# Three 256-column matmuls into one set of columns in the second layer of a two-layer block with experts

## The reference, cut to what matters

```python
h = gelu(einsum('bnd,hd->bnh', x, fc1_w) + fc1_b)
shared = einsum('bnh,sh->bns', h, fc2_w) + fc2_b
We = experts_w[indices]                      # one of 16 experts for each row
be = experts_b[indices]
expert_x = einsum('bnh,bph->bnp', h, We) + be[:, None, :]
out = x + concatenate([shared, expert_x], axis=-1)
```

## Time and profile before

| | |
|---|---|
| Three executions | 381.62, 382.38, 383.69 us |
| Span of the profiled execution (first to last instruction) | 380.7 us |
| TensorE (PE) matmuls busy | 368.8 us, 97% of the span, 1841 matmuls |
| TensorE weight loads (PEld) | 309.5 us, 1841 loads |
| VectorE (DVE) | 217.0 us, 57% |
| ScalarE (ACT) | 196.5 us, 52% |
| GpSimd (POOL) | 57.1 us, 15% |
| Mean granted TensorE clock | 0.985 |

### The profile page before, as it was taken

How to read it: one execution, slowest core, us unless ns; L and a number is a source line. 1 busy time by engine, 2 the same in 40 slices (tenths; PEclk the granted TensorE clock), 3 DMA queues, 4 the chain that set the end, 5 groups by cost and what they waited for, 6 DMA issues and landing times.

```text
span 380.7 us, 5936 instructions
## 1 busy us (share of the span) xinstructions
PE 368.8 (97%) x1841; PEld 309.5 (81%) x1841; DVE 217.0 (57%) x331; ACT 196.5 (52%) x266; POOL 57.1 (15%) x27
## 2 busy tenths in 40 slices
PE   4799999999999999999999999999999999999996
PEld 4587877888888888888888888888888888888885
DVE  1289477656556556655655665565565566556442
ACT  2297356555554655555455454546546554653520
POOL 1023121230120303012030300203030030302000
PEclk9599999999999999999999999999999999999999
DMA  6932987444240523324052441415234151300011
GB/s 137 250 77 85 305 149 196 144 104 126 60 141 26 140 88 96 131 58 143 27 133 94 96 131 46 127 54 134 94 89 138 43 130 55 89 28 29 28 37 47
DMA packets 64516, 39.08 MB, mean 103 GB/s; under 512 B 37338, under 2 KB 63722, under 8 KB 64506
## 3 DMA queue, kind: packets, MB, share of 16 engines
q1 hardware_dynamic: 63584, 35.41, 34.1%
q0 software_dynamic: 880, 3.54, 3.6%
q10 hardware_dynamic: 42, 0.00, 0.0%
HBM read 27.40 MB, written 8.39 MB: 94 GB/s over the span
## 4 chain that ended last, share of the span: by engine, by line
PE 86%; DVE 5%; DMA 5%; ACT 2%; SPq 2%; issue 1%
PE fc_ps L593 40%; PE acc_ps L629 29%; PE acc_ps L631 15%; DMA resid<-in_L_cond_fc_w 2%; DVE ht L466 2%; DMA pieces<-in_L_cond_experts_w 2%; SPq L174 1%; ACT ht L343 1%; PE fc_ps L601 1%; DVE tr_ps L411 1%; PE fc_ps L565 1%; ACT gelu L338 0%; SPq L218 0%; DVE xt L404 0%; ACT w2t L305 0%
## 5 line engine op out<-in xcount | busy, mean ns | idle before, releaser
L593 PE MATMUL fc_ps<-xt,w1t 128*128 128x512 f32 x762 | 194.2, 394 | 0.0
L629 PE MATMUL acc_ps<-w2t,ht 128*128 128x512 f32 x512 | 185.1, 398 | 1.3 <-DVE resid L485 0.8
L593 PEld LDWEIGHTS fc_ps<-xt,w1t 128*128 128x128 f32 x762 | 135.6, 188 | 28.8
L466 DVE TENSOR_TENSOR ht<-gelu,ht 128x1024 fp32r<-128x1024 f32 x64 | 83.2, 1301 | 130.2 <-ACT ht L343 130.2
L338 ACT ACTIVATE gelu<-fc_ps,b 128x512 f32<-128x512 f32 x128 | 88.2, 690 | 131.5 <-PE fc_ps L593 127.8
L631 PE MATMUL acc_ps<-w2t,ht 128*128 128x256 f32 x512 | 143.5, 280 | 0.0
L629 PEld LDWEIGHTS acc_ps<-w2t,ht 128*128 128x128 f32 x512 | 96.2, 188 | 26.0 <-DVE w2t L404 1.8
L631 PEld LDWEIGHTS acc_ps<-w2t,ht 128*128 128x128 f32 x512 | 96.6, 189 | 3.9
L260 POOL TENSOR_TENSOR resid<-x_in,bias 128x1024 f32<-128x1024 f32 x16 | 51.0, 3190 | 282.0 <-DMA out<-resid 251.5
L343 ACT ACTIVATE ht<-gelu 128x1024 fp32r<-128x1024 f32 x64 | 67.9, 1062 | 2.0
L481 DVE TENSOR_TENSOR resid<-acc_ps,resid 128x256 f32<-128x256 f32 x64 | 26.8, 419 | 7.5 <-PE acc_ps L631 7.5
(11 more groups left out here) (27 smaller groups left out, 35.3 us busy)
## 6 DMA issues: line engine op xcount, KB each, us to landing
x_in<-in_x SPq DMA_DIRECT2D x16, 512.0 KB, 4.6
pieces<-in_L_cond_experts_w SPq DMA_DIRECT2D x128, 64.0 KB, 2.0
out<-resid SPq DMA_DIRECT2D x30, 256.0 KB, 2.2
pieces<-in_x SPq DMA_DIRECT2D x56, 128.0 KB, 2.8
w2t<-w2t POOLq DMA_DIRECT2D x4, 768.0 KB, 8.6
resid<-in_L_cond_fc_w SPq DMA_DIRECT2D x8, 128.0 KB, 7.0
bias<-in_L_cond_experts_b SPq DMA_DIRECT2D x32, 32.0 KB, 3.5
pieces<-in_L_cond_fc_w SPq DMA_DIRECT2D x4, 192.0 KB, 4.9
```

The lines of the kernel that those rows point to most:

```text
L466: nc.vector.tensor_tensor(ht[:, par, LO, 2 * r:2 * r + 2, :].rearrange("p k t -> p (k t)"), gelu[:, r % 2, :], ht[:, par, HI, 2 * r:2 * r ...
L593: last = nc.tensor.matmul(fc1_ps[:, j % FC1_BANKS, :], w1t[:, d, w, js], xt[:, par, d, v, :], start=(at == 0), stop=(at == len(terms) - 1))
L629: nc.tensor.matmul(acc_ps[:, bank, :], ht[:, par, HI, k, ts], w2t[:, par, t // T, k, :], start=(k == 0), stop=False)
```

## The change

The second layer no longer uses two sets of columns. For each token tile and chunk three matmuls of 256 columns (HI by HI, HI by LO, LO by HI) add into columns 0 to 255 of the bank. The columns multiplied for a chunk stay 512 + 256 = 3 x 256. One addition instead of two drains a tile, and the semaphore between the two additions goes. VectorE gets waits on its own semaphore `tr_lo` ahead of the transposes into `tr_ps` in `step`; they ask for remainders computed earlier on the same engine.

```diff
@@ tile_out
                 dve.wait_ge(acc_filled, 1 + q + 1)
                 if t == 0:
                     dve.wait_ge(resid_ready, i + 1)
-                nc.vector.tensor_tensor(dst, acc_ps[:, bank, OUT:2 * OUT], dst, ALU.add)\
-                    .then_inc(cross_added, 1)
-
-                dve.wait_ge(cross_added, q + 1)
                 nc.vector.tensor_tensor(dst, acc_ps[:, bank, 0:OUT], dst, ALU.add)\
                     .then_inc(acc_drained, 1)
@@ step of VectorE
                     if r == 0 and x_ahead:
+                        dve.wait_ge(tr_lo, x_at(i))
                         x_square(par, None, 1, 1)
                     if r in (1, 2):
+                        dve.wait_ge(tr_lo, x_at(i) + r if x_ahead else x_at(i))
                         experts_square(1 - par, e_use, r - 1, r - 1)
                     if r == 3 and x_next:
+                        dve.wait_ge(tr_lo, e_at(i, x_ahead) + 1)
                         x_square(1 - par, x_use, 0, 0)
@@ stage3_half
                 ts = slice(t * P, (t + 1) * P)
+                dst = acc_ps[:, bank, 0:OUT]
                 for k in range(half * HALF, (half + 1) * HALF):
-                    nc.tensor.matmul(acc_ps[:, bank, :], ht[:, par, HI, k, ts],
-                                     w2t[:, par, t // T, k, :], start=(k == 0), stop=False)
-                    last = nc.tensor.matmul(acc_ps[:, bank, OUT:2 * OUT], ht[:, par, LO, k, ts],
-                                            w2t[:, par, t // T, k, 0:OUT],
+                    w_hi = w2t[:, par, t // T, k, 0:OUT]
+                    w_lo = w2t[:, par, t // T, k, OUT:2 * OUT]
+                    nc.tensor.matmul(dst, ht[:, par, HI, k, ts], w_hi, start=(k == 0), stop=False)
+                    nc.tensor.matmul(dst, ht[:, par, HI, k, ts], w_lo, start=False, stop=False)
+                    last = nc.tensor.matmul(dst, ht[:, par, LO, k, ts], w_hi,
                                             start=False, stop=(k == K - 1))
```

More of the change, by code:

```diff
@@ L129, in cond_mlp_residual @@
         resid_ready = sem("resid_ready")
-        cross_added = sem("cross_added")
         TR_X0, TR_X1, TR_E0, TR_FIRST = 0, 6, 8, 10
```

## The result

The changed kernel took 385.42 us (median of eight executions, 383.77 to 386.54), the kernel before 382.06 us (eight executions, 381.42 to 383.69). The ratio is 1.0081, 95% interval 1.0064 to 1.0098: 0.8% slower, some 3.1 us. The forecast was 385.6. The span of the profiled execution went from 380.7 to 383.8 us.

The account below looks back on a forecast made before the run. TensorE's matmul stream was taken as the bound: +3.7 us for longer halves less 0.46 at the end gives +3.2, from 382.38 to 385.6 us, 0.8% slower. The forecast's own range was 384.0 to 387.5; 8 in 10, 381.3 to 389.0.

Parts of the forecast that it names:

- What bounds the kernel: From 59.20 to 377.60 us only TensorE's matmuls count, so a change to its instruction stream is paid in full there.
- The price of the new stream: Second layer on TensorE: 12 matmuls of 256 columns priced like the float32 transposes, 1.431 us a half against 1.40, +0.031.
- How many halves pay: Of 128 halves, nine before 59.20 us are hidden in TensorE's waits; the other 119 pay, +3.7 us.
- without that cover: First nine halves: if TensorE's waits before 59.20 us did not hide their growth, it would add 0.3 us.
- The groups stay at 1.39: Groups of six 512-column matmuls keep their 1.39 us; a change of this would show the forecast wrong.
- The tail: End of the program: one of the two drain additions leaves the chain, -0.46 us.
- VectorE: 64 additions, 27 us of its 217, go without gain in the middle; VectorE ends near 190 us busy.
- only columns count: First rival, TensorE: the surplus is a share of columns, halves change by 0.00, span 381.9 us; chance 0.26.
- the third rival: TensorE: the weight load becomes the bound, 0.125 us a matmul, 393.8 us, halfway 389.5; chance 0.09.
- The second rival: TensorE: even streams run faster since changing widths may cost, 377.1 us, or 379.0 if the repeated load is skipped; chance 0.07.
- theory W: From the follow-ups, not the prediction: on TensorE, the first six 512s behind a run of 256s take 27 ns more in all.

Follow-up runs that it names:

- Run 7: The changed kernel with 64 tokens in place of 128 in the second layer's stationary operand, matmuls still 256 columns wide: one execution, 376.43 us.
- run 5: The changed kernel with the three matmuls of a chunk 128 columns wide in place of 256, loads and count unchanged: one execution, 374.20 us.
- run 3: The changed kernel with the order HI*HI, LO*HI, HI*LO in each chunk, so neighbours inside it never share a stationary operand: 384.97 us, ratio 1.0072.
- run 1: The kernel before with the second layer's 512-column matmul split into two of 256 in different columns, both additions kept: 385.32 us against 382.44, ratio 1.0077.
- run 11: The changed kernel with the first layer's 512-column matmuls also split into two of 256: one execution, 391.99 us.
- run 8: The changed kernel without the HI*LO matmul, 8 matmuls of 256 columns a half in place of 12: one execution, 329.10 us.
- run 6: The changed kernel with the three matmuls of a chunk 384 columns wide in place of 256: one execution, 467.85 us.
- run 2: The kernel before with its matmuls kept, but one addition draining a tile and the changed kernel's waits on `tr_lo`: 381.46 us, ratio 0.9983.
- run 4: The kernel before with the four 512-column matmuls of a half first, then its four 256-column ones: 379.66 us, ratio 0.9933.
- run 9: The kernel before with all eight 256-column matmuls of a tile moved behind its second half: 379.21 us against 382.20, ratio 0.9922.

## Why the prediction was right, point by point

**What bounds the kernel.** Right. From 59 us to the last matmul TensorE was busy throughout, in both kernels, and the change was paid in full there.

**The price of the new stream.** Right in size: 0.120 us a matmul, 1.43 a half, taken from the float32 transposes. Of its two parts one was wrong: I wrote that "one instruction costs 13 to 15 ns beyond its columns, whatever its width". Run 7 shows that an instruction has no such fixed price (13 ns with a load of 128 columns, 7 with one of 64), and run 5 that the sentence ends below some width: at 128 columns a matmul takes 0.112 and not 0.067. In this change every instruction had a full load and 256 columns, so the wrong owner gave the right sum. The repeated load of `ht` HI wasn't cheaper (run 3), and the shared columns cost nothing (runs 1 and 11). One reading was off without harm: at the lower clock the transposes start 0.213 apart and not 0.223, which takes in a first step of 0.283.

**How many halves pay.** Right. Nine halves ahead of 59 us were hidden: TensorE had stood waiting for 0.6 us ahead of the matmul at 59.40 in the changed kernel, and in run 8 it came at 58.86 though TensorE had 4 us less to do. The 0.2 us between 59.20 and 59.40 is no effect of the change that one could read: this point scatters from 57.62 to 59.40 over the traces. With halves longer by 0.65 the cover was gone (run 6), as the forecast's "without that cover" had it.

**The groups stay at 1.39.** Right for the six groups of a step that stand alone, off for the two at its start: in a row they took 2.78 and now 2.75. By the chain that is 0.036 us in each of some 14 steps, -0.5 us that the sum lacked, and the prediction had named a change of the groups' 1.39 as a sign against it. Together: 119 x 0.032 = +3.8 for the halves, -0.5 for the double groups, +0.1 in the other groups, +0.2 for the later start, -0.46 at the end makes 3.1, the growth of the span between the two profiled executions. That the forecast came within 0.2 us of the median is in part luck: what its sum lacked (-0.5, +0.1, +0.2) nearly cancels, and single executions of one kernel lie 2 to 3 us apart.

**The tail.** Right: -0.46 in the chain, -0.65 (-1.1 to -0.1) when done alone (run 2), with the waits on `tr_lo` in it, which the forecast had at nothing.

**VectorE.** Right that its time buys nothing. Wrong that it would fall to near 190 us: it was 212.7. The 27 us left, but `ht` LO grew by 22 (after; line, engine, op, count, busy us, mean ns, idle before):

```profile
L465 DVE TENSOR_TENSOR ht<-gelu,ht 128x1024 fp32r<-128x1024 f32 x64 | 105.7, 1652 | 137.3 <-ACT ht L342 137.3
L259 POOL TENSOR_TENSOR resid<-x_in,bias 128x1024 f32<-128x1024 f32 x16 | 38.4, 2397 | 299.5 <-DMA out<-resid 266.6
```

Before, the mean of the same two was 1301 and 3190 ns. The timeline shows the place where they meet, before and then after:

```profile
147.80 1.22 DVE L466 TENSOR_TENSOR ht<-gelu,ht 128x1024 fp32r<-128x1024 f32 x1 [2.37 <-ACT ht L343]
147.81 3.49 POOL L260 TENSOR_TENSOR resid<-x_in,bias 128x1024 f32<-128x1024 f32 x1 [18.83 <-DMA out<-resid]
```

```profile
148.38 2.40 POOL L259 TENSOR_TENSOR resid<-x_in,bias 128x1024 f32<-128x1024 f32 x1 [19.94 <-DMA out<-resid]
148.85 3.01 DVE L465 TENSOR_TENSOR ht<-gelu,ht 128x1024 fp32r<-128x1024 f32 x1 [2.86 <-ACT ht L342]
```

Whoever starts first runs at its usual length (1.22, 2.40), and the other takes longer than usual by about the time that was left to the first. GpSimd's addition waits for the store of the block before. Counted from the step's first group (143.16 before, 144.25 after), GpSimd starts at 4.65 before and at 4.13 after, VectorE at 4.64 and 4.60: with one addition fewer in the drain the store is earlier, so that GpSimd now comes first and VectorE is held, once a step. The Trainium skill says so in SBUF — State Buffer, section SBUF: two separate sides: VectorE and GpSimd share a pair of ports that the first one holds for its whole instruction; a VectorE operation with two SBUF inputs competes for it with a GpSimd operation that reads SBUF. Both are so here (`gelu` and `ht`; `x_in` and `bias`). The trace agrees, with the numbers above. I should have drawn this from the sum of the edits: what an earlier drain triggers. It cost nothing, since TensorE never waited for it after 59 us.

**The rivals.** That only columns count fell with the spacing of 0.120, and with run 6. A bound like the third rival's exists, at 0.112 us with a load of 128 columns (run 5; that it is the load's isn't shown), and lies just under what 256 columns take, so it never decided. (Halfway to that rival's 393.8 would be 389.7, not 389.5, which changes nothing.) The second rival was half right: changing widths does cost. Its price stands in run 4 (0.02 us a half) and in the groups behind narrow matmuls (0.03 each, 1.39 against six times 0.227). But the changed kernel kept the larger part of it, since each half of narrow matmuls still stands before a group of wide ones, and what it took away was less than the four new loads of each half (4 x 0.0133 = +0.053 against 0.032 measured; the other 0.021 is the alternation that went).

## What to carry to other kernels

On a path of back-to-back matmuls price the stream by starts: columns / 2.4 GHz, plus a toll for each matmul with its load (here 13 ns with 128 columns loaded, 7 with 64), and look for a row of the same shape before assuming that equal columns mean equal time. Splitting a wide matmul adds loads; saving additions on an engine that TensorE never waits for gives back only what stands at the program's end. Where all sums go to the same place in any order, as here, the order of widths is free to choose: putting wide matmuls beside wide and narrow beside narrow gained 0.7 to 0.8% without touching the work.

## What the runs showed that I had not expected

- **Widths next to each other.** Behind a change from narrow to wide the 512-column matmuls start 0.233, 0.236, 0.229, 0.232 and 0.231 us apart and then 0.227 (mean of the changed kernel's single groups). So six take 1.39 behind narrow ones, whether these number 4 (run 4) or 24, and also behind 384-column ones (run 6). A further six in a row take 1.36 in the changed kernel and in run 9, but 1.38 in run 4, 1.37 in run 6 and 1.40 in the kernel before, where the twelve take 2.78. How long the slow starts last thus depends on what stood before, and theory W's two values (1.36 and 1.39) hold in those two kernels and not in all. A 256-column matmul right behind wide ones is quicker (0.113, then 0.119, then 0.120). Alternating 512 and 256 in before had some 512s at 0.24. What in TensorE causes this, no run here tells; with one width throughout (run 11) it is gone.
- **The toll at the full clock only.** At the lower level (1.2 GHz, granted clock 0.50) the eight transposes at 12.17 start 0.283 us apart once and then 0.213 six times, and the 512-column matmuls behind them 0.427: the columns alone. That the toll vanishes there wasn't tested in a kernel of its own.
- **A faster engine let another one go first.** The held `ht` LO follows the drain: run 2, which changes the drain alone, has 1636 and 2426 ns for the pair of operations, run 1, which keeps both additions, 1373 and 3012. By their means the pair changes with the number of additions and not with the matmuls.
